# The experts' second product of a two-layer network, written as five products of rounded parts

## The reference

```python
def _swiglu(gu, inter):
    g, u = (gu[..., :inter], gu[..., inter:])
    return jax.nn.silu(g) * u
...
logits = jnp.einsum('th,eh->te', x, gate_w)              # E = 16 experts
topk_w, topk_idx = jax.lax.top_k(softmax(logits), K)     # K = 2 per token
gu = jnp.einsum('th,ehj->etj', x, w_gate_up)             # 256 -> 2*176
h = _swiglu(gu, I)                                       # I = 176
y = jnp.einsum('eti,eih,te->th', h, w_down, combine)     # 176 -> 256
y = y + _swiglu(x @ shared_gate_up, SI) @ shared_down    # dense part, SI = 352
```

## Time and profile before

| what | us |
|---|---|
| three runs | 506.21, 506.1, 516.81 |
| their median | 506.21 |
| span of the profiled execution | 506.1 |
| TensorE busy | 489.5 |
| VectorE busy | 342.6 |
| ScalarE busy | 297.2 |
| GpSimd busy | 275.6 |

### The profile page before, as it was taken

The page is one execution under the profiler, slowest core; times in us unless marked ns, Lnnn a source line. Parts: engine busy times, 40 slices in busy tenths (PEclk is TensorE's granted clock), DMA queues, the critical chain, the costliest instruction groups (busy, mean ns, idle before and its releaser), DMA issues.

```text
span 506.1 us, 7336 instructions
## 1 busy us (share of the span) xinstructions
PE 489.5 (97%) x2418; PEld 374.1 (74%) x2418; DVE 342.6 (68%) x732; ACT 297.2 (59%) x590; POOL 275.6 (54%) x253
## 2 busy tenths in 40 slices
PE   7999999989999999999999999999998999999997
PEld 5455557767887678879888888877766767677785
DVE  6999999898989999558989996224232322322347
ACT  5897898978899678589456343354331342323220
POOL 0163758749474566473634466847765665555500
PEclk9999999899999999999999999999999999999999
DMA  8900003004532011044105675722244222222177
GB/s 305 331 2 0 0 2 124 2 0 159 175 126 87 2 42 43 1 133 155 59 2 180 204 233 184 253 84 77 84 135 144 75 82 76 73 73 80 67 283 236
DMA packets 20245, 55.35 MB, mean 109 GB/s; under 512 B 3361, under 2 KB 6097, under 8 KB 20209
## 3 DMA queue, kind: packets, MB, share of 16 engines
q1 hardware_dynamic: 15696, 42.56, 24.7%
q0 software_dynamic: 4512, 12.33, 7.8%
HBM read 37.18 MB, written 17.74 MB: 109 GB/s over the span
## 4 chain that ended last, share of the span: by engine, by line
PE 71%; ACT 7%; POOL 6%; DMA 5%; issue 5%; DVE 4%; another core or an unknown queue 1%; SPq 0%; DVEq 0%; ACTq 0%
PE bank L317 50%; PE bank L510 9%; DMA y_rows<-m_y,dest 5%; PE bank L411 3%; POOL y_rows L1508 2%; POOL xg L1496 2%; PE bank L499 1%; PE bank L543 1%; PE bank L384 1%; ACT L643 1%; PE bank L570 1%; DVE m_y L1356 1%; PE bank L458 1%; ACT fd L729 1%; PE bank L400 1%
## 5 line engine op out<-in xcount | busy, mean ns | idle before, releaser
L1508 POOL DMA_INDIRECT y_rows<-m_y,dest x47 | 47.5, 1010 | 38.9 <-DVE m_y L1356 30.4
L1356 DVE TENSOR_SCALAR m_y<-bank,gslot 128x256 f32<-128x256 f32 x47 | 22.3, 483 | 61.1 <-DMA y_rows<-m_y,dest 36.6
L317 PE MATMUL bank<-mw,m_xt 128*128 x188 | 61.5, 463 | 0.8 <-DVE hs L1233 0.6
L1496 POOL DMA_INDIRECT xg<-xn_rows,tab x47 | 45.6, 971 | 20.2 <-issue 10.5
L317 PE MATMUL bank<-yhr,wsg_h 128*128 128x512 f32 x128 | 52.8, 412 | 0.0
L317 PE MATMUL bank<-hyr,wsg_h 128*128 128x512 f32 x128 | 50.0, 391 | 0.0
L317 PE MATMUL bank<-yhr,wsg_l 128*128 128x512 f32 x128 | 49.9, 390 | 0.0
L317 PE MATMUL bank<-mw,m_ht 88*128 x188 | 46.2, 381 | 3.1 <-DVE m_y L1356 2.0
L317 PEld LDWEIGHTS bank<-mw,m_xt 128*128 128x128 f32 x188 | 33.6, 189 | 17.8 <-issue 4.5
L1437 POOL TENSOR_TENSOR tk<-tk 128x512 f32<-128x512 f32 x16 | 21.0, 1315 | 38.0 <-ACT tk L787 37.9
L317 PEld LDWEIGHTS bank<-mw,m_ht 88*128 88x128 f32 x188 | 33.8, 190 | 8.7 <-issue 4.0
(11 more groups left out here) (272 smaller groups left out, 1393.5 us busy)
## 6 DMA issues: line engine op xcount, KB each, us to landing
mw<-in_gu SPq DMA_DIRECT2D x16, 352.0 KB
ga<-y_rows SPq DMA_DIRECT2D x8, 512.0 KB, 6.7
mw<-in_dn SPq DMA_DIRECT2D x16, 176.0 KB
wsg_w<-in_wsg SPq DMA_DIRECT2D x4, 512.0 KB, 4.2
spilled_x<-fa SPq DMA_DIRECT2D x4, 512.0 KB, 2.8
hx<-spilled_x SPq DMA_DIRECT2D x4, 512.0 KB, 4.6
xn_rows<-fg SPq DMA_DIRECT2D x4, 512.0 KB, 4.1
spilled_y<-fa SPq DMA_DIRECT2D x4, 512.0 KB, 3.0
```

Source lines behind the costliest of these rows:

```text
L317: mm = e.matmul(o, a, b, start=n == 0, stop=n == len(terms) - 1)
L1356: e.tensor_scalar(m_y[j % 3][:, :], ps("jd", j)[:, 0:D], gslot[:, j:j + 1], None, ALU.mult).then_inc(s["jy"], 1)
L1496: e.indirect_dma_start(out=xg[j % GATHERED][:, :], out_offset=None, in_=xn_d, in_offset=bass.IndirectOffsetOnAxis(ap=tab[:, j:j + 1], axis ...
L1508: e.indirect_dma_start(out=y_d, out_offset=bass.IndirectOffsetOnAxis(ap=dest[:, j:j + 1], axis=0), in_=m_y[j % 3][:, :], in_offset=None).t ...
```

## The change

The second product of each tile is written as five float32r products. The 176 rows of `h` are dealt out anew. Rows 0 to 127 are one piece of 128. Rows 128 to 175 stand twice in a second piece of 128, at 0 to 47 and at 64 to 111, with zeros between. Of the weights there are now three pieces of 256 columns: the high part and the low part of rows 0 to 127, and a third piece with the high part of rows 128 to 175 at 0 to 47 and the low part at 64 to 111. The product is high by high, high by low, low by high of the first piece, and high and low of `h` with the third.

- TensorE: `xdown` has five products in place of two; `hturn`'s transposes have 128 columns of weights in place of 88.
- VectorE: a new step `jhlow(j)` makes the low part of the turned `h`; `jtimes(j)` has one more small product of 48 columns; `mlow(n)` makes the low parts of the weights (two subtractions for each expert); `jpad()` writes the zeros.
- ScalarE: a new step `mround(n)` rounds the weights (128 x 512 for each expert); `jhcopy` writes 128 rows.
- SyncE: `dn` is now 128 rows of 512 in two pieces. It lands at a raw place, four of which turn for experts 0 to 6 and two for 7 to 15. So `experts(4)` to `(6)` wait for the `mlow` of four before, `experts(9)` to `(15)` for that of two before, and `experts(7)` for `mlow(6)` and for `tab` (`rt` at 22). All sixteen now wait for the spills of block 2, since the raw places of the first seven lie there.
- `jxcopy(0)`, `jpad` and the gathers from 5 on wait for the dense chunks 0 to 2 of block 3 (`past`), since their buffers now lie on those chunks' weights.
- The table `w_vec` is part of `w_cst`.
- The lists of all five engines are written anew. In TensorE's, `dup(3, 1)`, `dgate(3, 2)`, `dup(3, 2)` and `ddown(2, 10)` come ahead of `xup(0)`, and `dup(3, 5)` and `ddown(3, 4)` after the last `xdown`. In GpSimd's, thirteen `breathe` steps come ahead of the tiles and ten after the last scatter.

```diff
 def xdown(j, n):
     o = take(("jd", j), n, s["jy"], j + 1)
-    q.wait_ge(s["jtc"], j + 1)
+    if j == 0:
+        q.wait_ge(*low_of(E - 1))
+    q.wait_ge(s["x1"], 2 * NB + j + 1)
     r = place[j]
-    products(o[:, 0:D], [(m_ht[j % 3][:, c * P:(c + 1) * P], mw[0:88, bass.DynSlice(r + (704 + c * D), D)]) for c in range(2)]).then_inc(s["jd"], 1)
+    w, wl, wb = (mw_r[:, bass.DynSlice(r + (UW + k * D), D)] for k in range(3))
+    h, l = m_ht[j % 3]
+    terms = [(h[:, 0:P], w), (h[:, 0:P], wl), (l[:, 0:P], w), (h[:, P:2 * P], wb), (l[:, P:2 * P], wb)]
+    products(o[:, 0:D], terms).then_inc(s["jd"], 1)
...
+def mround(n):
+    q.wait_ge(d_mw[n % 2], 16 * STAGED.count(n % 2) + 32 * (n // 2 + 1))
+    o = n * EW + UW
+    hi = mw_r[:, o:o + 4 * D].rearrange("p (z n) -> p z n", n=2 * D)[:, :, 0:D]
+    e.activation(hi, raws[n], ACT.Copy).then_inc(s["ph"], 1)
...
 def jtimes(j):
     q.wait_ge(s["js"], j + 1)
-    e.tensor_tensor(m_h[j % 3][:, :], m_h[j % 3][:, :], ps("ju", j)[:, 176:352], ALU.mult).then_inc(s["jh"], 1)
+    if j > 2:
+        q.wait_ge(s["jt"], j - 2)
+    e.tensor_tensor(m_h[j % 3][:, 192:240], m_s[j % 3][:, 128:176], ps("ju", j)[:, 304:352], ALU.mult)
+    e.tensor_tensor(m_h[j % 3][:, 0:176], m_s[j % 3][:, :], ps("ju", j)[:, 176:352], ALU.mult).then_inc(s["jh"], 1)
+
+def jhlow(j):
+    q.wait_ge(s["jtc"], j + 1)
+    h, l = m_ht[j % 3]
+    e.tensor_tensor(l[:, :], ps("jt", j)[:, 0:D], h[:, :].bitcast(F32), ALU.subtract).then_inc(s["x1"], 1)
+
+def mlow(n):
+    q.wait_ge(s["ph"], len(PREP) + n + 1)
+    o = n * EW + UW
+    raw = raws[n]
+    b = mw_r[64:112, o + 2 * D:o + 3 * D]
+    e.tensor_tensor(mw_r[:, o + D:o + 2 * D], raw[:, 0, :], mw_r[:, o:o + D].bitcast(F32), ALU.subtract)
+    e.tensor_tensor(b, raw[64:112, 1, :], b.bitcast(F32), ALU.subtract).then_inc(low_of(n)[0], 1)
...
 def experts(n):
...
+    if n == EARLIER:
+        q.wait_ge(*low_of(n - 1))
+        q.wait_ge(s["rt"], 22)
+    elif n > EARLIER + 1:
+        q.wait_ge(*low_of(n - 2))
+    elif 3 < n < EARLIER:
+        q.wait_ge(*low_of(n - 4))
     if n > 1:
         q.wait_ge(d_mw[n % 2], 16 * STAGED.count(n % 2) + 32 * (n // 2))
     o = n * EW
-    e.dma_start(mw[:, o:o + 704], gu[n]).then_inc(d_mw[n % 2], 16)
-    e.dma_start(mw[0:88, o + 704:o + EW], dn[n]).then_inc(d_mw[n % 2], 16)
+    e.dma_start(mw[:, o:o + UW], gu[n]).then_inc(d_mw[n % 2], 16)
+    e.dma_start(raws[n], dn[n].rearrange("p (z n) -> p z n", z=2)).then_inc(d_mw[n % 2], 16)
```

More of the change, by code:

```diff
@@ L142, in build @@
         at[0] = top_at
[L143 to L146, removed]
+        at[0] = E * EW
+        assert at[0] >= top_at
+        at[0] += 2 * D
+        xg = [tile(f"xg{n}", D) for n in range(3)]
         assert at[0] <= top_at + 3072
@@ L194, in build @@
         g_i, g_f = tile("g_i", 32, U32), tile("g_f", 8)
-        m_xt.append(also("m_xt2", at[0], D))
-        m_ht.append(also("m_ht2", at[0] + D, D, parts=88))
+        xg[3:3] = [also(f"xg{n}", at[0] + (n - 3) * D, D) for n in range(3, 5)]
         hot, gval = tile("hot", 512), tile("gval", 32)
@@ L588, in tensor @@
[L588 to L611, removed]
@@ L612, in tensor @@
-            xup(2, 3); xturn(3, 5); hturn(0, 0); hturn(1, 1); xturn(4, 4); ddown(2, 10, 6, 7); hturn(2, 4); xturn(5, 5); xturn(6, 0); xup(3, 3)
-            xup(4, 5); xturn(7, 0); xup(5, 3); hturn(3, 5); xdown(0, 4); xdown(1, 2); hturn(4, 0); xdown(2, 5); xup(6, 4); xturn(8, 5); xturn(9, 3)
-            xturn(10, 2); dup(3, 1, 1); xdown(3, 0); xup(7, 5); hturn(5, 0); xup(8, 4); xturn(11, 3); xdown(4, 2); hturn(6, 5); hturn(7, 3)
-            xup(9, 0); xup(10, 5); xup(11, 4); xturn(12, 2); xdown(5, 5); xturn(13, 0); xturn(14, 2); hturn(8, 1); ddown(3, 0, 6, 7); hturn(9, 0)
@@ L616, in tensor @@
-            hturn(10, 2); xdown(6, 1); xdown(7, 5); xdown(8, 3); dgate(3, 2, 4); xup(12, 2); xup(13, 1); hturn(11, 3); xturn(15, 2); xturn(16, 5)
-            xup(14, 0); xup(15, 2); xdown(9, 1); xdown(10, 4); hturn(12, 3); hturn(13, 0); dup(3, 2, 5); hturn(14, 2); hturn(15, 0); xdown(11, 4)
-            xturn(17, 1); xturn(18, 5); xdown(12, 3); xdown(13, 4); ddown(3, 1, 6, 7); xdown(14, 3); xturn(19, 0); xturn(20, 5); xup(16, 1)
-            xup(17, 2); xup(18, 0); dgate(3, 3, 4); dgate(3, 4, 1); dup(3, 3, 3); xdown(15, 0); hturn(16, 2); xup(19, 5); xturn(21, 2); xturn(22, 0)
@@ L620, in tensor @@
-            ddown(3, 2, 6, 7); xdown(16, 0); hturn(17, 4); hturn(18, 2); xup(20, 1); xup(21, 0); xturn(23, 5); xdown(17, 1); hturn(19, 4)
-            hturn(20, 5); xdown(18, 2); xdown(19, 4); xup(22, 1); hturn(21, 4); xturn(24, 2); xturn(25, 0); xup(23, 3); xup(24, 5); xup(25, 2)
-            hturn(22, 3); xdown(20, 5); xturn(26, 1); xturn(27, 0); xdown(21, 4); xturn(28, 1); xup(26, 5); xturn(29, 2); xturn(30, 1); hturn(23, 4)
-            hturn(24, 0); xup(27, 3); xup(28, 0); xup(29, 1); hturn(25, 3); hturn(26, 5); dup(3, 4, 2); xdown(22, 4); xdown(23, 0); xdown(24, 2)
@@ L628, in tensor @@
-            xdown(33, 0); xup(39, 3); xup(40, 1); xdown(34, 5); xdown(35, 2); xdown(36, 0); xturn(42, 5); xturn(43, 4); xup(41, 2); hturn(37, 4)
-            hturn(38, 5); dgate(3, 5, 3); xup(42, 2); xup(43, 1); hturn(39, 5); xturn(44, 0); xdown(37, 4); xdown(38, 5); hturn(40, 2); hturn(41, 0)
-            xdown(39, 4); ddown(3, 4, 6, 7); xturn(45, 0); xturn(46, 5); xdown(40, 4); xdown(41, 2); hturn(42, 3); xup(44, 4); xup(45, 1)
-            xup(46, 5); hturn(43, 4); hturn(44, 1); hturn(45, 0); xdown(42, 3); xdown(43, 5); xdown(44, 1); hturn(46, 3); dup(3, 5, 0); xdown(45, 3)
@@ new lines, in tensor @@
+            ddown(2, 2, 6, 7); ddown(2, 3, 6, 7); dup(2, 5, 0); routed(7); dup(2, 6, 5); dup(2, 7, 1); dup(2, 8, 4); dgate(2, 7, 0); ddown(2, 4, 6, 7)
+            ddown(2, 5, 6, 7); dgate(2, 8, 2); dup(2, 9, 3); dgate(2, 9, 0); dgate(2, 10, 5); ddown(2, 6, 6, 7); ddown(2, 7, 6, 7); dgate(3, 0, 1); dgate(3, 1, 2)
+            dup(2, 10, 0); dup(3, 0, 4); ddown(2, 8, 6, 7); ddown(2, 9, 6, 7); dgate(3, 2, 3); xturn(0, 5); xturn(1, 0); dup(3, 1, 1); dup(3, 2, 4)
+            ddown(2, 10, 6, 7); xup(0, 5); xturn(2, 0); xturn(3, 2); ddown(3, 0, 6, 7); xturn(4, 0); xturn(5, 2); xup(1, 1); xup(2, 3); xup(3, 4); xturn(6, 0)
@@ new lines, in tensor @@
+            xdown(8, 0); xdown(9, 2); xdown(10, 4); dgate(3, 3, 3); xdown(11, 0); xdown(12, 2); hturn(13, 1); hturn(14, 5); xup(15, 4); xup(16, 0); xup(17, 3)
+            dgate(3, 4, 2); xturn(18, 1); xturn(19, 5); xturn(20, 4); xturn(21, 0); xturn(22, 3); hturn(15, 1); xup(18, 5); xup(19, 2); xdown(13, 4); xdown(14, 0)
+            dup(3, 3, 5); hturn(16, 3); hturn(17, 4); hturn(18, 0); xdown(15, 1); xup(20, 5); xup(21, 1); xturn(23, 3); hturn(19, 4); xdown(16, 2); xturn(24, 5)
+            dup(3, 4, 3); hturn(20, 1); hturn(21, 2); xdown(17, 5); xdown(18, 0); xturn(25, 4); xup(22, 3); xup(23, 5); xturn(26, 0); xturn(27, 1); xdown(19, 2)
@@ L636, in scalar @@
+            xdown(42, 3); xturn(46, 5); xdown(43, 4); hturn(45, 0); xup(46, 1); xdown(44, 5); xdown(45, 3); hturn(46, 2); xdown(46, 4); dgate(3, 6, 0)
+            dup(3, 5, 1); ddown(3, 4, 6, 7); dup(3, 6, 5); dgate(3, 7, 3); dgate(3, 8, 2); dgate(3, 9, 4); dup(3, 7, 1); dup(3, 8, 0); ddown(3, 5, 6, 7)
+            ddown(3, 6, 6, 7); ddown(3, 7, 6, 7); dup(3, 9, 5); dup(3, 10, 3); dgate(3, 10, 1); ddown(3, 8, 6, 7); ddown(3, 9, 6, 7); ddown(3, 10, 6, 7)
         @block.scalar
@@ L1529, in sync @@
+            breathe(20); breathe(21); breathe(22)
         @block.sync
```

400 lines of the change are left out of this document (235 added, 165 removed).

## The result

The changed kernel took 522.95 us (median of 4, 522.32 to 525.61) beside 506.68 for the kernel before: a ratio of 1.0306, 95% interval 1.0259 to 1.0353. It is 3% slower, and 19 us above the forecast of 504. Its profiled execution has a span of 521.7 us.

What follows compares the result with a forecast made beforehand. TensorE was taken to bound the kernel, with GpSimd nearly equal among the tiles: `xup(0)` at 348, plus 116.6 of work, 10 of waits, 27.2 and 2.8 of tail, less 0.4, gives 504.2 us; range 492 to 517.

Steps and rivals of the forecast that it cites:

- I take the 10 us of waits of before: Experts' stage: 10 us of waits, as in the kernel before, added to TensorE's 116.6 us of work.
- GpSimd sets the pace: Rival, experts' stage: GpSimd's 117 us with waits that can't be caught up; waits become 16 us, time 510; chance 0.16.
- Five products in 0.60 us: Each tile's `xdown`: five float32r products at 0.119 us each, 0.60 in all, in place of 0.87.
- The last rival: Rival, `xdown`: register-addressed products run at 0.217 us each, costing 10 us instead of saving 13, some 525; chance 0.05.
- Tail 30.0 us: From the last `xdown` to the end: 27.2 us as before plus 2.8 for `dup(3, 5)` and `ddown(3, 4)`.
- `tab` at 313.5, issue at 314: Ahead of the tiles: seven `mlow`, 5 us, delay `tab` from 308.1 to 313.5; the next load is issued at 314.
- Turns of 7.4 us: Expert loads after `tab`: four turns of two loads with rounding, 7.4 us each, 29.6 in all, to 343.6.
- TensorE due at `xup(0)` at 336.9, waits 11, starts at 348: Ahead of the tiles: TensorE ready at 336.9 waits 11 us for the last load, landing at 348.
- Saving 12.9 us: TensorE's work in the tiles: the cheaper `xdown` saves 0.275 us in each of 47 tiles, 12.9 us.
- The roundings choke the loads: Rival, expert loads: roundings and contention make each turn 10.8 us, `xup(0)` at 364, time 520; chance 0.15.
- `w_vec`, 0.4 us: At the start: merging `w_vec` saves one place in the DMA queue, about 0.4 us, between 0 and 1.
- a TensorE that waits more than 15 us within the tiles: Experts' stage: one of the signs named beforehand that would show the forecast wrong; 10 us of waits were forecast.

Runs made afterwards that it cites:

- after_b: The changed kernel, unaltered, run on chip 4: 500.17 us.
- after_reg: The changed kernel with the tiles in a regular order in all engines' lists, on chip 1: 499.71 us, ratio 0.989 to the kernel before.
- nohop: The changed kernel without `jhlow`, the high part of `h` used for the low one, on chip 1: 497.31 us, ratio 0.9839 to the kernel before.
- noturn: The changed kernel with `dn` loaded to its final place, no load waiting for `mlow` or `tab`, weights' low part zero, chip 1: 496.67 us, ratio 0.9814.

## Why the prediction was wrong

**The step that failed** is "I take the 10 us of waits of before" for the experts' stage. On the first chip they were 32.6 us, of which some 20 are idle time of TensorE (148.70 less 128.95 busy), on chip 6 26.2. The stage took 148.7 us instead of 126.6. The step before it named the right resource: GpSimd's 117 us of indirect DMAs beside TensorE's 116.6. What I priced was GpSimd's own pitch, some 1.3 us, and that held: on the first chip a train of three starts at 365.55, 366.86 and 368.15, on chip 4 at 365.80, 367.09 and 368.36. What I could not see in the earlier trace rows is that on some chips signals of other engines come late while those DMAs go out close together. The kernel before has two in 3.15 us, the changed one asks for two in 2.46, and on those chips a tile with all its gathers takes 2.92 to 3.03. That lies nearest to the rival "GpSimd sets the pace", with 23 us more of waits where I gave it 6. But its mechanism isn't that one: GpSimd begins an indirect DMA every 1.70 us in tiles 10 to 40 of the first chip and is busy for only 85.1 of the stage's 148.7 us. Why signals come late around those DMAs stays open.

On chips that hold no signals the same step was right: 7.0 and 6.2 us of waits instead of 10, and 500.5 and 500.2 us for the forecast of 504.2.

**Point by point.**
- *Five products in 0.60 us*, 0.119 each with addressed weights: right on all chips. The last rival falls.
- *Tail 30.0 us*: 30.1. Right.
- *`tab` at 313.5, issue at 314*: issue at 311.30 on the first chip, 314.5 on chip 4. An `mlow` took 0.42 + 0.42 where I had 0.42 + 0.33. *Turns of 7.4 us*: 6.34, 6.80, 5.88, 5.54. Too dear by 1.3 a turn: rounding and subtractions (1.5 us) hide beside the other load of the pair more than I took. The last load is issued at 335.86 instead of some 343.
- *TensorE due at `xup(0)` at 336.9, waits 11, starts at 348*: starts at 342.9 on the first chip, 346.7 to 347.0 on three others. That 348 was near is luck in part: the last load was issued 4 to 8 us earlier than forecast but took some 6 us to land and not 4.4 (landed at 341.75 and 345.51, first chip and chip 4), and `xup(0)` started 0.9 and 1.2 us after the later of its load and TensorE's chunks, which I had not priced. TensorE itself came to that point only at 341.97 and 344.90, not at 336.9, since 250 to 310 lost 7 to 9 us in place of 2.3, partly at half clock (PEclk 0.94 in chip 4's row). I had priced the new lists ahead of the tiles at nothing. So loads and TensorE arrived nearly together, and TensorE stood idle only 0.9 and 1.8 us right before `xup(0)`.
- *Saving 12.9 us*: right in TensorE's work. On chip 4 the stage went from 147.2 to 122.1, 25.1 us less: 12.7 on the tiles, 8.3 for chunks that only changed sides (together the 137.6 - 116.6 of the prediction), the rest, some 4, fewer waits, 10.6 to 6.2. The first `xup` came 15.3 us later and the tail is 3.0 longer; 25.1 - 15.3 - 3.0 is the 6.8 us between the spans, 505.7 and 498.9.
- *The roundings choke the loads*: no. The first subtraction of `mlow` took 0.42 to 0.68 us in the chain above. The price by contention does show where GpSimd subtracts at the same time, but that is seldom. On chip 4 (`after_b`):

```profile
318.92 1.26 DVE L1409 TENSOR_TENSOR mw_r<-raw,mw_r 128x256 fp32r<-128x256 f32 x1 [3.03 <-ACT mw_r L927]
...
318.59 1.30 POOL L1543 TENSOR_TENSOR hxr<-hx,xhr 128x512 fp32r<-128x512 f32 x1
```

There the same subtraction took 1.26 us in place of 0.42 and ended 0.29 us after GpSimd's. In the turns, the 0.68 on the first chip is one such case, and chip 4 has two more, of 0.95 and 1.09; beside GpSimd's memsets and indirect DMAs it took 0.41 to 0.49. The rule of the Trainium skill (SBUF — State Buffer, "Who interferes with whom"), that VectorE with two SBUF inputs contends with a GpSimd instruction that reads SBUF, agrees with these rows; what was too dear was a meeting in every turn.
- *`w_vec`, 0.4 us*: can't be told from the spread of the runs.
- The sign of failure that I gave, "a TensorE that waits more than 15 us within the tiles", is the one that came.

## What to carry to other kernels

When a change shortens the time between indirect DMAs, or fills a queue that was slack, price the interval that they leave to the rest, and time the kernel on several chips before its verdict is believed: one chip gave 1.031 and another 0.987, with intervals far apart. Ask of a big loss first whether an unaltered run on another chip has it: `after_reg`, `nohop` and `noturn` each looked like the cure until one was made. And try a plain regular order before a costly rewrite of the arithmetic: it gave the kernel before some 5 us (ratio 0.9891), on a chip that holds no signals; elsewhere it is untried.

## What the runs showed of the hardware

- Chips differ in kind. On the first one and on 6, 14 and 15 TensorE's signals come late, 64 to 91 of 487 in the changed kernel and its variants; on 1, 4, 7 and 9 none or one. The kernel before hardly shows it in its time, 506.7 to 508.9 us against 504.5 to 507.2, though 60 of its signals are late on the first chip. On the first chip ScalarE's and VectorE's signals are late too (37 of 542, 39 of 634). In the held places several come through at once, as those of 371.07, 371.67 and 371.89 (two `xdown` and an `xturn`), which come between 372.76 and 372.87. What path they share with the indirect DMAs no run here shows, nor why the chips differ.
- TensorE's granted clock fell to half (1.2 GHz) for 6.8 us from 349.8 on the first chip, behind a pause of 2.3 us that had ended at 348.7. In it two `xup` took 5.00 us (351.83, x8 in the chain) where two at 360.57, at full clock, took 2.37. Further stretches of 3.4 us stand at 319.1 and 401.0. On chip 4 one of 6.8 us stands at 297.0. So the pause at 348.7 was paid for twice, once idle and once in slower products.
